# The odd slots' groups of x are loaded from ScalarE's queue, the even ones from SyncE's

## The chip, the cores and the metric

The kernel runs on one core of one Trainium2 chip. The metric is the device time of one execution in microseconds (us); what is compared is the median of several executions.

## The reference: what is computed

The input x has 1024 samples of 12500 numbers (float32, 51.2 MB). The reference is a factorization machine with a small network beside it:

```python
x_reg = input_data @ W_lin.T + b_lin                     # 1024 x 1
emb = input_data @ factors                               # 1024 x 16
sum_squared = jnp.square(emb.sum(axis=1))
squared_sum = (jnp.square(input_data) @ jnp.square(factors)).sum(axis=1)
h = jax.nn.relu(emb @ W1.T + b1)                         # 128 wide
h = jax.nn.relu(h @ W2.T + b2)                           # 64 wide
dnn_out = h @ W3.T + b3
x = x_reg + 0.5 * (sum_squared - squared_sum)[:, None] + dnn_out
x = 0.5 + jax.nn.sigmoid(x) * 5.0
```

Every number of x is needed twice: as it is, against 17 columns of weights (16 factors and W_lin), and squared, against one column of weights (the sums of the squared factors).

## The kernel before, in words

x comes transposed, 12500 rows of 1024 samples. It is read once, in this order: 128 first rows (xf), 84 remaining rows (xl), then 22 groups of 512 rows (2 MB each), then 1024 last rows (xe) in six pieces (PIECES, line 38: 1024, 1024, 1024, 512, 256 and 256 KB). In a group each of the 128 partitions gets 4 rows of x in one run of 16 KB (CHUNKS = 4); in a piece of xe it gets runs of 2 KB per row and half of the samples, so 8, 8, 8, 4, 2 and 2 KB.

The groups go through a ring of four slots of xr (RING = 4, group g in slot g % 4). The loops are written as 5 rounds of four slots (ROUNDS = 5; round 0 stands ahead of the loop, rounds 1 to 4 are the loop) and a rest of two groups, 20 and 21 (PART = 2). For each group:

- SP issues its load (line 172) into the slot of group g - 4. It waits for lin_used (TensorE has multiplied g - 4) and for squared (ScalarE has squared g - 4). The first four loads (line 166) wait for nothing. After the last load SP issues the six pieces of xe (line 184) with no wait at all, since xe has memory of its own.
- TensorE multiplies the group by its weights (multiply, line 426: 16 matmuls into p_lin) and then adds the fourth chunk of the squares of the group before (squares_before, line 416: 16 matmuls into p_tot).
- ScalarE squares the group into one of two buffers sq (square, line 234: two instructions at line 242 of 128 x 2048). It waits for the landing, and for VectorE and TensorE to be done with the squares of g - 2.
- VectorE adds three of the four chunks of squares, weighted, to acc (line 341).
- GpSimd copies the weights of the group into the ring wr (lines 196 and 204).

Each engine takes the groups in their order. At the start ScalarE's queue issues the loads of the weights w, of the last weights and of params (lines 223 to 225); after that only SP's queue is used. After group 21 TensorE's order is written out by hand (lines 517 to 550): the pieces of xe one after the other, and between them the squares, the two layers of the network and the sums for the two halves of the samples. The two stores of y (line 189) are SP's.

Of the kernel before, what the change touches and what calls it, by code (L numbers as in the profile page):

```python
# [22 lines left out]
RING = 4  # L23
# [3 lines left out]
PART = GROUPS - ROUNDS * RING  # L27
# [29 lines left out]
def fm_kernel(nc, xT, x_end, w_all, w_last, params, out):  # L57
    x_first = xT[0:P, :]
    x_rest = xT[P:P + REST, :]
    x_groups = xT[P + REST:, :].rearrange("(g p c) b -> g p (c b)", p=P, c=CHUNKS)  # L60
    out_rows = out.rearrange("(h t b) -> h t b", h=2, t=4)

    with ExitStack() as ctx:
        def sb(name, shape, dt=F32):
            return ctx.enter_context(nc.sbuf_tensor(name, shape, dt))
# [4 lines left out]
        def sem(name):  # L70
            return ctx.enter_context(nc.semaphore(name))
# [3 lines left out]
        xr = sb("xr", [P, RING, CHUNKS, B])  # L75
# [32 lines left out]
        x_landed = [sem(f"x_landed{s}") for s in range(RING)]  # L108
# [11 lines left out]
        squared = sem("squared")  # L120
        first_squared = sem("first_squared")
        added = sem("added")
        lin_used = sem("lin_used")
# [19 lines left out]
        def group(r, s):  # L143
            return RING * r + s

        def adds_by(g, c):

            return 2 + ADDS * g + c + 1
# [4 lines left out]
        def end_sq(h, c, n):  # L153

            return sq[:, h].rearrange("p c b -> p (c b)")[:, c * HALF:(c + n) * HALF]

        def by_vector(n):

            return 1 if n > 1 else 0

        @block.sync
        def _(sp):
            sp.dma_start(xf[:, :], x_first).then_inc(first_landed, 16)  # L163
            sp.dma_start(xl[0:REST, :], x_rest).then_inc(rest_landed, 16)  # L164
            for s in range(RING):
                sp.dma_start(xr[:, s].rearrange("p c b -> p (c b)"), x_groups[s]).then_inc(x_landed[s], 16)  # L166

            def load(r, s):

                sp.wait_ge(lin_used, group(r - 1, s) + 1)  # L170
                sp.wait_ge(squared, 2 * group(r - 1, s) + 2)
                sp.dma_start(xr[:, s].rearrange("p c b -> p (c b)"),  # L172
                             x_groups[bass.ds(group(r, s), 1)].rearrange("g p n -> (g p) n")
                             ).then_inc(x_landed[s], 16)

            with sp.Fori(1, ROUNDS) as r:
                for s in range(RING):
                    load(r, s)
            for s in range(PART):
                load(ROUNDS, s)  # L180
            at = 0
            for i, (h, c, n) in enumerate(PIECES):
                rows = x_end[at:at + P * n * HALF].rearrange("(p m) -> p m", p=P)
                sp.dma_start(xe[:, h, c:c + n, :].rearrange("p c b -> p (c b)"), rows).then_inc(end_landed[i], 16)
                at += P * n * HALF

            for h in range(2):
                sp.wait_ge(y_ready, h + 1)
                sp.dma_start(out_rows[h], y[0:P:32, h, :]).then_inc(y_stored, 16)
            sp.wait_ge(y_stored, 32)  # L190
# [30 lines left out]
        @block.scalar  # L221
        def _(act):
            act.dma_start(w[:, :, :].rearrange("p c k -> p (c k)"), w_all).then_inc(w_landed, 16)
            act.dma_start(wl[0:REST, :], w_last).then_inc(wl_landed, 16)
            act.dma_start(pr[:, :], params).then_inc(pr_landed, 16)

            act.wait_ge(zero_set, 1)
            nc.scalar.activation(warm[:, :], zero[:, 0:1], ACT.Sigmoid)  # L228
            act.wait_ge(first_landed, 16)
            nc.scalar.activation(sqf[:, :], xf[:, :], ACT.Square).then_inc(first_squared, 1)  # L230
            act.wait_ge(rest_landed, 16)
            nc.scalar.activation(sql[0:REST, :], xl[0:REST, :], ACT.Square).then_inc(first_squared, 1)

            def square(r, s):
                g = group(r, s)
                act.wait_ge(x_landed[s], 16 * (r + 1))
                if type(r) is not int or g >= SQ:

                    act.wait_ge(added, adds_by(g - SQ, ADDS - 1))
                    act.wait_ge(sq_used, g - SQ + 1)  # L240
                for c in range(0, CHUNKS, 2):
                    nc.scalar.activation(sq[:, s % SQ, c:c + 2, :], xr[:, s, c:c + 2, :],  # L242
                                         ACT.Square).then_inc(squared, 1)

            for s in range(RING):
                square(0, s)
            with act.Fori(1, ROUNDS) as r:
                for s in range(RING):
                    square(r, s)
            for s in range(PART):  # L250
                square(ROUNDS, s)

            def square_end(i):
                h, c, n = PIECES[i]
                n -= by_vector(n)
                act.wait_ge(end_landed[i], 16)
                if c == 0:

                    g = GROUPS - SQ + h
                    act.wait_ge(added, adds_by(g, ADDS - 1))  # L260
                    act.wait_ge(sq_used, g + 1)
                nc.scalar.activation(end_sq(h, c, n), xe[:, h, c:c + n, :].rearrange("p c b -> p (c b)"),  # L262
                                     ACT.Square).then_inc(end_squared, 1)

            def copy_lin(h):
                act.wait_ge(p_lin_done, h + 1)
                for u in range(2):
                    nc.scalar.copy(lin[:, h, u, :], p_lin[h][:, u * QUART:(u + 1) * QUART]).then_inc(lin_ready, 1)  # L268

            def layer1(h):  # L270
                act.wait_ge(p_h1_done, 2 * h + 1)
                nc.scalar.activation(h1[:, h, 0, :], p_h1[0][:, 0:QUART], ACT.Relu,
                                     bias=pr[:, C_B1:C_B1 + 1]).then_inc(h1a_ready, 1)

            def layer2(h):
                act.wait_ge(p_h2_done, 2 * h + 1)
                nc.scalar.activation(h2[0:H2, h, :], p_h2[0:H2, 0:QUART], ACT.Relu,  # L277
                                     bias=pr[0:H2, C_B2:C_B2 + 1]).then_inc(h2a_ready, 1)

            def embedding_square(h):  # L280
                act.wait_ge(p_es_done, h + 1)
                nc.scalar.activation(gsq[:, h, :], p_es[:, 0:EIGHTH], ACT.Square).then_inc(gsq_ready, 1)

            def sigmoid(h):
                act.wait_ge(p_tot_done, h + 1)
                nc.scalar.activation(sg[:, h, :], p_tot[h][:, 0:EIGHTH], ACT.Sigmoid,  # L286
                                     bias=bias[:, :]).then_inc(sg_ready, 1)

            square_end(0)
            square_end(1)  # L290
            copy_lin(0)
            act.wait_ge(pr_landed, 16)
            square_end(2)
            layer1(0)
            embedding_square(0)
            square_end(3)
            layer2(0)
            square_end(4)
            act.wait_ge(bias_ready, 1)
            sigmoid(0)  # L300
            copy_lin(1)
            layer1(1)
            embedding_square(1)
            layer2(1)
            sigmoid(1)
# [287 lines left out]
```

## Time and profile before

| | us |
|---|---|
| median of 3 executions | 141.06 (140.56 to 141.28) |
| the profiled execution | 141.34 |
| its span, first to last instruction on the core | 139.6 |
| TensorE matmuls busy | 91.5 |
| VectorE busy | 96.8 |
| ScalarE busy | 94.6 |
| GpSimd busy | 19.8 |
| moved by DMA | 52.26 MB, mean 374 GB/s over the span |

The profiled execution is one of its own, 0.28 us above the median; 1.74 us of it lie outside the span. Busy times are sums over the span. In the rows below the engines are PE (TensorE's matmuls), PEld (its weight loads), DVE (VectorE), ACT (ScalarE), POOL (GpSimd) and SP (SyncE); a q behind the name means the engine's instruction queue, where DMAs are issued. L172 is line 172 of the kernel.

### The profile page before, as it was taken

To read this page: it belongs to the slowest core of one execution; us is meant where nothing else is said; L and a number is where in the kernel's file an instruction comes from. 1 tells how busy PE (TensorE), PEld (TensorE's weight loads), DVE (VectorE), ACT (ScalarE), POOL (GpSimd) and SP (SyncE) were. 2 spreads that over 40 slices of the span, in tenths; PEclk is the share of its full clock that TensorE was granted. 3 is DMA by queue.
4 is the path that set the end of the run, shared out by engine and by line. 5 is a ranking of instruction groups with operands and counts; after the bars stand their busy time and mean duration, and the time that the engine had idled before them with its cause. 6 is when DMAs were issued, how large, how long until landed. Compare 5 with 4: busy or idle time off the path is not lost.

```text
span 139.6 us, 2634 instructions
## 1 busy us (share of the span) xinstructions
PE 91.5 (66%) x989; PEld 30.8 (22%) x989; DVE 96.8 (69%) x86; ACT 94.6 (68%) x65; POOL 19.8 (14%) x48
## 2 busy tenths in 40 slices
PE   6067852972964655964765647576574772999991
PEld 1010111220221211220221212112121120446650
DVE  0063798779678739778777977977797797796321
ACT  3050876966886656876696687669669776997341
POOL 0053002012022203022120220312022000000000
PEclk9999999599599685698698697579779789689999
DMA  4999999999999999999999999999999999992000
GB/s 89 377 371 412 446 418 418 441 432 404 432 446 418 418 437 434 399 437 446 413 418 451 423 409 446 441 409 427 446 413 418 451 425 402 423 396 79 5 8 1
DMA packets 4683, 52.26 MB, mean 374 GB/s; under 512 B 616, under 2 KB 752, under 8 KB 1476
## 3 DMA queue, kind: packets, MB, share of 16 engines
q1 hardware_dynamic: 4290, 51.21, 87.3%
q10 hardware_dynamic: 386, 0.95, 2.4%
q8 instruction: 5, 0.08, 0.2%
q14 instruction: 2, 0.02, 0.0%
HBM read 52.15 MB, written 0.00 MB: 374 GB/s over the span
## 4 chain that ended last, share of the span: by engine, by line
DMA 69%; ACT 14%; PE 12%; SPq 1%; issue 1%; ACTq 0%; DVE 0%
DMA xr<-in_xT 69%; ACT sq L242 13%; PE p_tot L392 5%; PE p_lin L392 5%; PE p_h L475 2%; PE p_h L506 1%; ACT sg L286 1%; PE p_es L485 0%; SPq L164 0%; ACT h L277 0%; SPq L163 0%; SPq L166 0%; SPq L172 0%; ACT lin L268 0%; DVE y L374 0%
## 5 line engine op out<-in xcount | busy, mean ns | idle before, releaser
L242 ACT ACTIVATE sq<-xr 128x2048 f32<-128x2048 f32 x44 | 81.6, 1903 | 30.0 <-DMA xr<-in_xT 29.0
L341 DVE SCALAR_TENSOR_TENSOR acc<-sq,wr,acc 128x1024 f32<-128x1024 f32 x66 | 84.9, 1286 | 23.2 <-ACT sq L242 20.6
L392 PE MATMUL p_lin<-xr,wr 128*17 128x512 f32 x352 | 57.4, 784 | 39.0 <-DMA xr<-in_xT 34.8
L204 POOL COPY wr<-s_all 128x4 f32 (+1 forms) x22 | 14.1, 639 | 74.4 <-PE p_tot L392 62.7
L392 PEld LDWEIGHTS p_lin<-xr,wr 128*17 128x17 f32 x352 | 9.5, 108 | 67.5 <-issue 41.5
L392 PE MATMUL p_tot<-sq,wr 128*1 128x128 f32 x352 | 17.4, 325 | 0.0
L392 PEld LDWEIGHTS p_tot<-sq,wr 128*1 128x1 f32 x352 | 11.9, 103 | 22.9 <-issue 22.1
L196 POOL COPY wr<-w 128x68 f32 (+1 forms) x22 | 6.8, 309 | 13.0 <-DMA w<-in_w_all 7.7
L392 PE MATMUL p_lin<-xf,w 128*17 128x512 f32 x4 | 3.6, 1052 | 4.9 <-DMA xf<-in_xT 4.9
L313 DVE SCALAR_TENSOR_TENSOR fsq<-w 128x1552 f32<-128x1552 f32 x1 | 1.8, 1776 | 7.0 <-DMA w<-in_w_all 7.0
L262 ACT ACTIVATE sq<-xe 128x1536 f32<-128x1536 f32 (+1 forms) x5 | 5.6, 1134 | 0.5 <-issue 0.5
L392 PE MATMUL p_lin<-xe,w 128*17 128x512 f32 (+2 forms) x48 | 5.3, 514 | 0.0
L230 ACT ACTIVATE sqf<-xf 128x1024 f32<-128x1024 f32 x1 | 1.1, 1058 | 4.6 <-DMA xf<-in_xT 4.6
L359 DVE SCALAR_TENSOR_TENSOR sq<-xe,s_all 128x512 f32<-128x512 f32 x5 | 3.7, 748 | 0.2
L392 PE MATMUL p_lin<-xl,wl 84*17 84x512 f32 x4 | 3.6, 1055 | 0.0
L392 PE MATMUL p_tot<-sq,s_all 128*1 128x128 f32 x88 | 3.3, 273 | 0.0
L369 DVE TENSOR_SCALAR h<-p_h,pr 64x256 f32<-64x256 f32 x2 | 1.0, 490 | 3.3 <-PE p_h L506 3.3
L228 ACT ACT_TABLE_LOAD x1 | 1.3, 1283 | 2.3 <-issue 2.3
L392 PEld LDWEIGHTS p_tot<-sq,s_all 128*1 128x1 f32 x88 | 2.3, 84 | 1.6 <-issue 1.0
L277 ACT ACTIVATE h<-p_h,pr 64x256 f32<-64x256 f32 x2 | 0.9, 468 | 2.5 <-PE p_h L506 2.5
L475 PE MATMUL p_h<-lin,pr 128*128 128x256 f32 x8 | 2.3, 405 | 0.1
L374 DVE TENSOR_SCALAR y<-sg 128x128 f32<-128x128 f32 x2 | 0.5, 226 | 2.2 <-ACT sg L286 2.2
(43 smaller groups left out, 27.7 us busy)
## 6 DMA issues: line engine op xcount, KB each, us to landing
xr<-in_xT SPq DMA_DIRECT2D x22, 2048.0 KB, 15.6
xe<-in_x_end SPq DMA_DIRECT2D x3, 1024.0 KB, 19.7
w<-in_w_all ACTq DMA_DIRECT2D x1, 824.5 KB, 7.4
xf<-in_xT SPq DMA_DIRECT2D x1, 512.0 KB, 7.6
xe<-in_x_end SPq DMA_DIRECT2D x1, 512.0 KB, 22.5
xe<-in_x_end SPq DMA_DIRECT2D x2, 256.0 KB, 22.8
xl<-in_xT SPq DMA_DIRECT2D x1, 336.0 KB
pr<-in_params ACTq DMA_DIRECT2D x1, 101.5 KB, 12.5
```

What stands on the lines that cost most here:

```text
L196: nc.gpsimd.tensor_copy(wr[:, s, :, 0:LIN], w[:, bass.ds(at, CHUNKS), :]).then_inc(wr_ready, 1)
L204: nc.gpsimd.tensor_copy(wr[:, s, :, LIN:WC].rearrange("p c k -> p (c k)"), s_all[:, bass.ds(at, CHUNKS)]).then_inc(wr_ready, 1)
L228: nc.scalar.activation(warm[:, :], zero[:, 0:1], ACT.Sigmoid)
L242: nc.scalar.activation(sq[:, s % SQ, c:c + 2, :], xr[:, s, c:c + 2, :], ACT.Square).then_inc(squared, 1)
L262: nc.scalar.activation(end_sq(h, c, n), xe[:, h, c:c + n, :].rearrange("p c b -> p (c b)"), ACT.Square).then_inc(end_squared, 1)
L286: nc.scalar.activation(sg[:, h, :], p_tot[h][:, 0:EIGHTH], ACT.Sigmoid, bias=bias[:, :]).then_inc(sg_ready, 1)
L313: nc.vector.scalar_tensor_tensor(fsq[:, :, :], w[:, :, 0:EMB], -0.5, w[:, :, 0:EMB], ALU.mult, ALU.mult).then_inc(fsq_ready, 1)
L341: nc.vector.scalar_tensor_tensor(acc[:, :], sq[:, s % SQ, c, :], wr[:, s, c, LIN:WC], acc[:, :], ALU.mult, ALU.add).then_inc(added, 1)
L359: nc.vector.scalar_tensor_tensor(end_sq(h, c, 1), xe[:, h, c, :], s_all[:, W_END + c:W_END + c + 1], xe[:, h, c, :], ALU.mult, ALU.mult).t ...
L392: return nc.tensor.matmul(out, lhsT, rhs, start=False, stop=False, skip_group_check=True)
L475: nc.tensor.matmul(p_h1[u][:, 0:QUART], pr[:, C_W1:C_W1 + H1], lin[:, h, u, :], start=True, stop=True).then_inc(p_h1_done, 1)
L506: nc.tensor.matmul(p_h2[u * H2:(u + 1) * H2, 0:QUART], pr[:, C_W2:C_W2 + H2], h1[:, h, u, :], start=True, stop=True).then_inc(p_h2_done, 1)
```

## The change

The nine loads of the odd slots that lie in the ring (groups 5, 7, 9, ... 21) are taken from SP and issued by ScalarE. SP keeps the even slots (groups 4, 6, ... 20), and behind them, as before, xe. On ScalarE the refill of slot 1 stands after the square of slot 2, the refill of slot 3 after the square of slot 0 of the next round; each waits for the same two counts as before. All else is as it was.

```diff
--- before.py
+++ after.py
@@ -173,10 +173,11 @@
                              x_groups[bass.ds(group(r, s), 1)].rearrange("g p n -> (g p) n")
                              ).then_inc(x_landed[s], 16)
 
+
             with sp.Fori(1, ROUNDS) as r:
-                for s in range(RING):
+                for s in range(0, RING, 2):
                     load(r, s)
-            for s in range(PART):
+            for s in range(0, PART, 2):
                 load(ROUNDS, s)
             at = 0
             for i, (h, c, n) in enumerate(PIECES):
@@ -242,11 +243,25 @@
                     nc.scalar.activation(sq[:, s % SQ, c:c + 2, :], xr[:, s, c:c + 2, :],
                                          ACT.Square).then_inc(squared, 1)
 
-            for s in range(RING):
+            def load(r, s):
+
+                act.wait_ge(lin_used, group(r - 1, s) + 1)
+                act.wait_ge(squared, 2 * group(r - 1, s) + 2)
+                act.dma_start(xr[:, s].rearrange("p c b -> p (c b)"),
+                              x_groups[bass.ds(group(r, s), 1)].rearrange("g p n -> (g p) n")
+                              ).then_inc(x_landed[s], 16)
+
+            for s in range(3):
                 square(0, s)
+            load(1, 1)
+            square(0, 3)
             with act.Fori(1, ROUNDS) as r:
-                for s in range(RING):
-                    square(r, s)
+                square(r, 0)
+                load(r, 3)
+                square(r, 1)
+                square(r, 2)
+                load(r + 1, 1)
+                square(r, 3)
             for s in range(PART):
                 square(ROUNDS, s)
```

## Rows read from the trace of the kernel before

**Rows 1.** The page, busy times by engine and the DMA slices.

```profile
PE 91.5 (66%) x989; PEld 30.8 (22%) x989; DVE 96.8 (69%) x86; ACT 94.6 (68%) x65; POOL 19.8 (14%) x48
DMA  4999999999999999999999999999999999992000
```

**Rows 2.** By stretches: length, busy (x instructions) per engine, PE clock, DMA share, GB/s.

```profile
40.00:66.00 26.00, 15.80 (x164) 4.79 (x156) 19.51 (x16) 18.65 (x11) 4.97 (x10) 0.79 1.00 423
66.00:92.00 26.00, 17.35 (x172) 5.41 (x168) 19.83 (x16) 20.08 (x12) 4.86 (x10) 0.76 1.01 432
```

**Rows 3.** ScalarE in order of time: start, length, instructions, idle before and its releaser.

```profile
64.93 3.71 ACT L242 ACTIVATE sq<-xr 128x2048 f32<-128x2048 f32 x2 [1.21 <-DMA xr<-in_xT]
...
118.62 3.71 ACT L242 ACTIVATE sq<-xr 128x2048 f32<-128x2048 f32 x2 [1.19 <-DMA xr<-in_xT]
```

**Rows 4.** The chain that ended last, its end: start, length, what.

```profile
102.96 15.64 DMA xr<-in_xT
...
118.64 2.52 PE p_lin L392 x16
...
137.33 0.23 DVE y L374
```

**Rows 5.** Pieces of xe: issues, first and last one's landing, first and last multiplication.

```profile
103.35 2.80 SPq L184 DMA_DIRECT2D xe<-in_x_end  x6
...
DMA to landing us min/median/max: 17.7/17.7/17.7
...
DMA to landing us min/median/max: 22.8/22.8/22.8
...
121.77 1.77 PE L392 MATMUL p_lin<-xe,w 128*17 128x512 f32 x8
...
132.28 0.41 PE L392 MATMUL p_lin<-xe,w 128*17 128x128 f32 x8
```

**Rows 6.** The start: issues in time, landings (page, part 6; last: first group of x).

```profile
0.74 0.40 ACTq L223 DMA_DIRECT2D w<-in_w_all  x1
0.75 0.40 SPq L163 DMA_DIRECT2D xf<-in_xT  x1
...
1.72 2.38 SPq L166 DMA_DIRECT2D xr<-in_xT  x4
1.88 0.35 ACTq L225 DMA_DIRECT2D pr<-in_params  x1
...
w<-in_w_all ACTq DMA_DIRECT2D x1, 824.5 KB, 7.4
xf<-in_xT SPq DMA_DIRECT2D x1, 512.0 KB, 7.6
pr<-in_params ACTq DMA_DIRECT2D x1, 101.5 KB, 12.5
...
DMA to landing us min/median/max: 12.9/12.9/12.9
```

**Rows 7.** TensorE in time: one group at full clock, one mostly at half.

```profile
59.98 1.91 PE L392 MATMUL p_lin<-xr,wr 128*17 128x512 f32 x16 [0.95 <-DMA xr<-in_xT]
61.71 0.62 PE L392 MATMUL p_tot<-sq,wr 128*1 128x128 f32 x16
...
86.67 1.11 PE L392 MATMUL p_tot<-sq,wr 128*1 128x128 f32 x16
...
99.15 3.49 PE L392 MATMUL p_lin<-xr,wr 128*17 128x512 f32 x16 [2.55 <-DMA xr<-in_xT]
```

**Rows 8.** Stretches at the start and the end, columns as in rows 2.

```profile
1.50:2.00 0.50, 0.50 (x2) 0.15 (x1) 0.00 (x0) 0.00 (x0) 0.00 (x0) 1.00 1.36 158
...
116.20:139.60 23.40, 17.96 (x320) 9.41 (x320) 13.13 (x17) 14.26 (x20) 0.00 (x0) 0.93 0.44 179
119.90:123.20 3.30, 3.30 (x32) 1.21 (x28) 2.47 (x2) 3.30 (x3) 0.00 (x0) 0.50 1.00 415
128.00:128.50 0.50, 0.50 (x20) 0.39 (x16) 0.09 (x1) 0.50 (x2) 0.00 (x0) 1.00 0.01 4
```

## Prediction

> **What bounds the kernel now.** I read the page's slices first: the DMA row stands at 9 or more from the second slice to the 36th, while VectorE and ScalarE are at 69% and 68% [rows 1]. Then the table by stretches: in the four stretches of 26 us from 14 to 118 us the DMA engines move 423 to 432 GB/s, and their share is never under 1.00 [rows 2]. Third, ScalarE's instructions in order of time: it squares each group for 3.71 us and then waits 1.15 to 1.2 us for the next one, so groups of 2 MB land every 4.89 us ((118.62 - 64.93) / 11) [rows 3]. The chain of waits says the same and adds the end: up to 118.6 us it is transfers of x, from then on TensorE, piece on piece, with ScalarE and VectorE in between, to 137.3 us [rows 4]. TensorE shows no idle there worth the name, and the pieces of the last rows (xe) have landed before it gets to them: the first is there at 103.35 + 17.7 = 121.05 us and is multiplied at 121.77; the last is issued at 103.35 + 2.80 - 0.43 = 105.7, is there 22.8 us later at 128.5 and is multiplied at 132.28 [rows 5]. So two things set the time: whether the DMA engines ever stand idle, and **when group 21, the last group of x, lands** (118.6 us). What follows that landing takes 18.9 us and moves with it.
>
> **The change, part by part.**
>
> *What is removed and added.* SP loses 9 of its 18 loads inside the ring (groups 5, 7, ... 21); ScalarE gets them, each as two waits and one issue. An issue occupied ScalarE's queue for 0.40 us for w and 0.35 for params [rows 6]. Nine times 0.4 is 3.6 us on ScalarE. It idles about 1.2 us per group, 2.4 us per pair of groups [rows 3], and the load stands after the second of the pair, so I price it at 0; without that idle it would be at most 3.6 us. The two waits are for squares that ScalarE itself has finished and for TensorE's multiplications of a group that landed a whole group earlier: TensorE needs 1.91 us at full clock and 3.4 to 3.5 us at half for them [rows 7], less than 4.89, so they too cost 0.
>
> *What moves.* In the old order the slot of group g is refilled when g has been squared. An odd slot is now refilled one group later: 7 after square 4, 9 after square 6, and so on, at the same moment at which SP refills the even slot. So loads go out in pairs, (7,8), (9,10) ... (19,20), 21 alone. Before, three loads were under way at each issue and a load took 15.6 us to land [rows 4]; now about two are.
>
> *How two queues share the DMA engines.* Only the start of the trace shows it. w and xf are issued at 0.74 and 0.75 us on different queues, both in 128 rows (824.5 KB and 512 KB, so 6.4 and 4 KB a row), and land 7.4 and 7.6 us later: together, although one is 1.6 times the other. params (0.8 KB a row) is issued at 1.88 and lands 12.5 us later at 14.4; the first group of x (16 KB a row), issued at 1.72, lands 12.9 later at 14.6 [rows 6]. Two transfers with the same number of rows end together whatever their bytes: the engines take turns row by row. By equal bytes params would have been through some 6 us earlier. I take turns by rows.
>
> *Steady state.* The members of a pair have 128 rows each, so they land together, every 2 x 4.89 = 9.78 us. Does the queue run dry? A pair lands at 0; ScalarE squares both, 7.45 us; its waits and those of SP add 0.15; then a latency L passes around the moving of bytes; and the new pair needs 9.78 us to move. That pair is due two periods later, at 19.56 (it is (g+3, g+4), with (g+1, g+2) between). So 17.4 + L must stay under 19.56, or L under 2.2 us. The rows bound L: the first bytes move in the half microsecond from 1.5 to 2.0, about 1.0 us after the issue, and the last ones between 128.0 and 128.5, when the last piece lands [rows 5, 8]: together some 1.5 us for the slowest of the engines. Counted by mean bytes the other end is higher: from 116.2 us to the end the stretch moves 23.4 x 179 = 4.19 MB, which is all of xe, so the mean engine is through with group 21 at 116.2, and it lands at 118.6: a lag of 2.4, which with the 1.0 makes L = 3.4 [rows 4, 8]. But in the half microsecond before the last landing 4 GB/s still move [rows 8], a hundredth of the full rate: one engine or a few are some 2 us behind the others, and it is the slowest, never dry itself, that sets a landing. So I take L = 1.5 and 0 us of empty queue, with 0.7 us in hand per pair, and keep (3.4 - 2.2) x 4 = 4.8 us as the other end (19.56 us is one cycle of the ring; there are four).
>
> *The end.* SP no longer waits for group 21: right after group 20 it issues all of xe, so xe stands in SP's queue behind 20 while 21 stands in ScalarE's behind 19. Groups 19 and 20 land together when all bytes up to 20 have moved, as before at 118.6 - 4.9 = 113.7 us. Then 21 (128 rows of 16 KB) takes turns with the first piece of xe (128 rows of 8 KB): 3072 KB have to move for both to be through, 1.5 x 4.89 = 7.33 us. Group 21 lands at 121.05 us: **+2.4 us**. The bound below is 0 (21 goes first, as now), the bound above 2.4 more (equal bytes, two pieces beside it: 2 x 4.89 after 113.7 is 123.5).
>
> *Is TensorE ready by then?* It gets 19 and 20 at once. A group costs 1.91 + 0.62 = 2.5 us at full clock and 3.4 + 1.1 = 4.5 us at half [rows 7]: it is through at 118.8 or at 122.7, so between 0 and 1.6 us late at 121.05. The trace alternates between the two levels, group by group, which gives 120.7: 0. ScalarE is through at 113.7 + 7.45 = 121.15: 0.1 late. I take 0.4 for both. After that the 18.9 us of [rows 4] follow unshortened; pieces of xe that lie ready earlier don't help, since TensorE was busy anyway.
>
> Here a rule of the Trainium skill speaks against any change in bandwidth: "DMA: Bandwidth & Descriptors", section "Issuing engines are not separate DMA queues", says that issuing from several engines only saves the sequencer's issue time. The traces agree as far as 1.00 of share leaves nothing to win [rows 2]; the order of arrival, on which my sum rests, that rule leaves open.
>
> *Sum.* The profiled execution took 141.34 us for a span of 139.6. 141.34 + 2.4 + 0.4 = 144.1; it lies 0.28 above the median of 141.06, so against the median **143.9 us**.
>
> **The rivals.**
>
> *Equal bytes* (chance 0.13): +2.4 more at the end, 146.3 us. For it: nothing but simplicity; against it params and w [rows 6].
>
> *The ring runs dry* (0.17): L is nearer to 3.4 than to 1.5, because the engines' lead over one another, now covered by three loads in flight, is lost each time a pair is used up. It decides from L = 2.2. Price 1 to 4.8 us on top: 144.9 to 148.7, middle 146.8.
>
> *Whole transfers by turns, so no change* (0.15): if a queue keeps the engines for one whole transfer before the other gets its turn, then the members of a pair land 4.89 us apart as now, the late refill is still covered (at each issue two groups less ScalarE's 3.85 us and the latency, some 4 us of work, are queued), and group 21 has its turn before the second piece at the latest: 0 to +2.4, and with 19, 20 and 21 having been issued in the order of now mostly 0, so 141.1 us. Against it: params would then not have needed as long as a group of x [rows 6]. The same page, section "Queues, rings and completion order", has the engines change queues after a packet of typically 9 to 17 descriptors; with 8 rows and a completion per engine that would be a whole transfer of this kernel, and 141.1 us.
>
> *A faster end* (0.05): the time falls if group 21 is not later and TensorE is granted the full clock after it. It runs at half (1.2 GHz) from about 119.9 to 123.2 us [rows 8], 3.3 us of work that would take 1.65 at 2.4 GHz: 141.06 - 1.65 = 139.4 us. It decides only where 21 stays at 118.6 and TensorE has idled longer ahead of it. Nothing in the rows makes both likely.
>
> **How the numbers follow.** Forecast 0.50, equal bytes 0.13, dry ring 0.17, no change 0.15, faster 0.05. The forecast's own range is 142.9 (nothing but half of the delay is missed) to 145.3 (TensorE at half clock, 1.6 for 0.4). The range for 8 in 10 takes in the no-change case and reaches into the dry ring: 141.0 to 147.5. Half a percent is 0.7 us, about what a measurement of this kernel can tell. Under 140.4: the faster case and a little, 0.06. Within: the no-change case less its tail, 0.14. Above: 0.80.
>
> **What the profile after should show.** Landings of x in pairs: ScalarE squaring two groups back to back (7.4 us), then idle about 2.3 us, instead of 1.2 us after each. Group 4 is late (about +4 us), since 5 shares its time. The DMA row stays at 9. Group 21 squared from about 121.1; the first piece of xe landed by then, some 20 us after its issue around 101. DMA's last bytes stay where they are, near 128 us. The prediction is wrong if groups still come every 4.89 us (turns by transfer), if gaps show in the DMA row ahead of the landings of pairs (L too small), or if 21 lands at 123.5 (equal bytes).

## The result, and the profile after

| | before | after |
|---|---|---|
| median, us | 141.09 (140.56 to 141.28, 4 runs) | 142.88 (142.46 to 143.49, 4 runs) |
| the profiled execution, us | 141.34 | 142.91 |
| its span, us | 139.6 | 140.8 |

The ratio is 1.0137, with a 95% interval of 1.0102 to 1.0171: 1.8 us slower, clear of noise. The forecast was 143.9 us with a range of 141.0 to 147.5.

The page of the kernel after, busy times and DMA slices, answers to [rows 1]:

```profile
PE 91.1 (65%) x989; PEld 30.5 (22%) x989; DVE 96.7 (69%) x86; ACT 94.3 (67%) x65; POOL 21.6 (15%) x48
DMA  4999999999999999999999999999999999980000
```

The table by stretches answers to [rows 2] (stretch, its length, busy time and instructions of each engine, PE clock, DMA share, GB/s):

```profile
40.00:66.00 26.00, 18.31 (x188) 5.93 (x180) 21.21 (x17) 20.82 (x12) 6.47 (x12) 0.79 1.00 424
66.00:92.00 26.00, 15.28 (x168) 4.84 (x172) 20.75 (x17) 19.19 (x11) 4.72 (x10) 0.86 1.01 432
```

Nothing is lost on the way: 424 and 432 GB/s for 423 and 432, the share is 1.00 or 1.01, no slice has a gap before the end. The bytes arrive as fast as before. What differs is whose bytes. ScalarE in order of time, kernel after, in the middle and at the end (as [rows 3]):

```profile
62.00 3.71 ACT L243 ACTIVATE sq<-xr 128x2048 f32<-128x2048 f32 x2 [1.17 <-DMA xr<-in_xT]
66.91 1.91 ACT L243 ACTIVATE sq<-xr 128x2048 f32<-128x2048 f32 x1 [1.20 <-DMA xr<-in_xT]
67.28 0.34 ACTq L250 DMA_DIRECT2D xr<-in_xT  x1
...
110.94 3.71 ACT L243 ACTIVATE sq<-xr 128x2048 f32<-128x2048 f32 x2 [1.16 <-DMA xr<-in_xT]
115.69 3.71 ACT L243 ACTIVATE sq<-xr 128x2048 f32<-128x2048 f32 x2 [1.05 <-DMA xr<-in_xT]
119.84 3.71 ACT L243 ACTIVATE sq<-xr 128x2048 f32<-128x2048 f32 x2 [0.43 <-PE p_tot L407]
```

Two things stand here that I hadn't expected. First, the load in ScalarE's queue (67.28) goes out 0.37 us after the square ahead of it has *begun*, not after it has ended at 70.6: the count that the load waits for was reached 1.2 us before the square began, and the queue runs ahead of the engine. The odd slot is refilled 1.6 us after its own square ended (62.00 + 3.71 = 65.7). Before, SP issued group 21's load at 102.96 ([rows 4]), 0.07 us after the square that it waited for, of group 17 (kernel before):

```profile
99.18 3.71 ACT L242 ACTIVATE sq<-xr 128x2048 f32<-128x2048 f32 x2 [1.15 <-DMA xr<-in_xT]
```

So the refill is 1.5 us later than it was, not a whole group. Second, the groups therefore don't arrive in pairs. They come every 4.9 us as before; the two queues are half a group apart, each with its own group half moved when the other one's lands. The trace's records of single DMA packets, of which each is one row of a group, show it: when the last row of group 20 had moved (114.56 us), 69 of the 128 rows of group 21 had moved too.

They are late by half a group, though, from group 8 on: group 10 is squared from 66.91, before from 64.93 [rows 3] (2.0 us, and about half a microsecond more without the late start explained below). At the end that lag has a price. Group 20 is in at 115.65 instead of 113.7 us, and 21 has come before 20 is dealt with. VectorE and TensorE in order of time show what that does; first the kernel before, then the kernel after (start, length, instructions, idle before):

```profile
115.73 4.06 DVE L341 SCALAR_TENSOR_TENSOR acc<-sq,wr,acc 128x1024 f32<-128x1024 f32 x3 [0.77 <-ACT sq L242]
120.62 4.07 DVE L341 SCALAR_TENSOR_TENSOR acc<-sq,wr,acc 128x1024 f32<-128x1024 f32 x3 [0.83 <-ACT sq L242]
124.61 2.31 DVE L359 SCALAR_TENSOR_TENSOR sq<-xe,s_all 128x512 f32<-128x512 f32 x3
...
125.41 0.40 PE L392 MATMUL p_tot<-sq,ones 128*1 128x128 f32 x8
```

```profile
117.69 8.26 DVE L356 SCALAR_TENSOR_TENSOR acc<-sq,wr,acc 128x1024 f32<-128x1024 f32 x6 [0.79 <-ACT sq L243]
125.87 2.07 DVE L374 SCALAR_TENSOR_TENSOR sq<-xe,s_all 128x512 f32<-128x512 f32 x3
...
123.69 0.62 PE L407 MATMUL p_tot<-sq,wr 128*1 128x128 f32 x16 [1.00 <-ACT sq L243]
...
126.67 0.40 PE L407 MATMUL p_tot<-sq,ones 128*1 128x128 f32 x8 [0.85 <-DVE sq L374]
...
138.59 0.23 DVE L389 TENSOR_SCALAR y<-sg 128x128 f32<-128x128 f32 x1 [0.88 <-ACT sg L301]
```

After, the additions of groups 20 and 21 are one row of six without a gap. VectorE's product of the first piece of xe starts 1.26 us later (125.87 for 124.61), TensorE waits 0.85 us for it, and from there all is 1.26 us later to the last instruction (138.59 for 137.33 in [rows 4]). In front of it TensorE, which bounded the old end, now has 1.00 + 0.85 = 1.85 us of idle. The 1.00 is ScalarE's: it squares 20 and 21 nearly back to back, too.

The chain of waits of the kernel after names another cause:

```profile
101.41 24.17 DMA xe<-in_x_end
125.63 0.24 issue
125.87 0.75 DVE sq L374
```

It follows VectorE's product back to a piece of xe that landed at 125.58. But VectorE shows no idle there; it was adding until 125.95. Nor does its first product read that piece: it needs the first one, which was in at 100.47 + 20.1 = 120.6, and the one of 125.58 is the third. A wait that ends while its engine is busy with something else is no cause.

1.26 us of the span against 1.8 us of the medians: the profiled execution of before had a late start. Its first group was squared from 14.62 us; among the thirteen kernels profiled here, variants with unchanged starts included, that instruction began between 13.86 and 14.62, mostly near 14.0, and at 14.07 in the kernel after. The 0.55 us belong to the executions, not to the change; 1.26 + 0.55 = 1.8. A profile that started at 13.89 us, of a kernel with all loads on SP and the time of the kernel before (late refill in one queue, below), gives the same without that addition:

```profile
113.36 3.71 ACT L242 ACTIVATE sq<-xr 128x2048 f32<-128x2048 f32 x2 [1.02 <-DMA xr<-in_xT]
124.24 2.30 DVE L359 SCALAR_TENSOR_TENSOR sq<-xe,s_all 128x512 f32<-128x512 f32 x3
136.95 0.23 DVE L374 TENSOR_SCALAR y<-sg 128x128 f32<-128x128 f32 x1 [0.88 <-ACT sg L286]
```

Beside it the kernel after squares group 20 2.33 us later (115.69), starts VectorE's product 1.63 us later (125.87) and its last instruction 1.64 us later (138.59).

### The profile page after: what moved, and what is told of

Same layout as the page of the kernel before. It is cut to its first block, busy times and chain, and to the rows that moved or that the text cites. A ratio compares the mean times of both kernels' runs of the same rounds, so it can differ in the third digit from the quotient of the medians.

```text
span 140.8 us, 2636 instructions
## 1 busy us (share of the span) xinstructions
PE 91.1 (65%) x989; PEld 30.5 (22%) x989; DVE 96.7 (69%) x86; ACT 94.3 (67%) x65; POOL 21.6 (15%) x48
## 4 chain that ended last, share of the span: by engine, by line
DMA 73%; ACT 9%; PE 7%; issue 5%; SPq 2%; ACTq 2%; DVE 1%; DVEq 0%
DMA xr<-in_xT 55%; DMA xe<-in_x_end 17%; ACT sq L243 8%; PE p_tot L407 3%; PE p_h L490 2%; ACTq L250 1%; PE p_lin L407 1%; PE p_h L521 1%; SPq L185 1%; DVE sq L374 1%; ACT sg L301 1%; SPq L172 0%; PE p_es L500 0%; ACT h L292 0%; SPq L164 0%
## 5 line engine op out<-in xcount | busy, mean ns | idle before, releaser
L205 POOL COPY wr<-s_all 128x4 f32 (+1 forms) x22 | 14.7, 667 | 76.2 <-PE p_tot L407 53.7
L407 PEld LDWEIGHTS p_tot<-sq,wr 128*1 128x1 f32 x352 | 11.6, 103 | 24.0 <-issue 22.4
L197 POOL COPY wr<-w 128x68 f32 (+1 forms) x22 | 8.1, 368 | 11.3 <-DMA w<-in_w_all 7.3
L407 PE MATMUL p_lin<-xe,w 128*17 128x512 f32 (+2 forms) x48 | 4.5, 451 | 0.0
L407 PE MATMUL p_tot<-sq,ones 128*1 128x128 f32 x40 | 2.0, 272 | 0.8 <-DVE sq L374 0.8
## 6 DMA issues: line engine op xcount, KB each, us to landing
xr<-in_xT SPq DMA_DIRECT2D x13, 2048.0 KB, 15.6
```

The lines of the kernel that those rows point to most:

```text
L197: nc.gpsimd.tensor_copy(wr[:, s, :, 0:LIN], w[:, bass.ds(at, CHUNKS), :]).then_inc(wr_ready, 1)
L205: nc.gpsimd.tensor_copy(wr[:, s, :, LIN:WC].rearrange("p c k -> p (c k)"), s_all[:, bass.ds(at, CHUNKS)]).then_inc(wr_ready, 1)
L407: return nc.tensor.matmul(out, lhsT, rhs, start=False, stop=False, skip_group_check=True)
```

## The experiments

**The refill really a group late (late refill).** ScalarE's load waits for the square ahead of it, which is what I had taken the change to do.

```diff
-                act.wait_ge(squared, 2 * group(r - 1, s) + 2)
+                act.wait_ge(squared, 2 * group(r - 1, s) + 4)
```

> ScalarE's load waits for the square that stands ahead of it in the program (the group after the one whose slot it refills), so that the odd refill really goes out a whole group late, at the moment of the even one, as my prediction had assumed of the change itself. Turns by rows and the prediction's sum: from group 7 on the groups land in pairs 9.8 us apart, ScalarE squares two back to back and idles 2.3 us, group 20 lands where it does before the change (113.7), group 21 at about 121.0, the end 2.4 to 2.9 us later than before: 143.5 to 144.0 us. Rival, equal bytes: 21 at 123.5, 146 us. Rival, the ring runs dry: gaps in the DMA row before a pair lands, over 145 us. Rival, lateness of the refill is of no effect: groups every 4.9 us and 142.9 us as with the change.

Measured: 154.1 us, ratio 1.093 (1.087 to 1.099). The page's DMA slices of this kernel:

```profile
DMA  4999999999999999799999899999599999960000
```

and its ScalarE in order of time:

```profile
83.94 0.37 ACTq L250 DMA_DIRECT2D xr<-in_xT  x1
86.61 3.71 ACT L243 ACTIVATE sq<-xr 128x2048 f32<-128x2048 f32 x2 [2.86 <-DMA xr<-in_xT]
90.48 3.71 ACT L243 ACTIVATE sq<-xr 128x2048 f32<-128x2048 f32 x2 [0.15 <-PE p_tot L407]
94.39 0.36 ACTq L250 DMA_DIRECT2D xr<-in_xT  x1
```

The pairs are there, two squares back to back; but a pair comes every 11.2 us (from 53.6 to 120.6 us six times), not every 9.8, and the slices show holes. The dry ring came true. The forecast of 143.9 us stood on a picture of the kernel that, once built, takes 154.1: 13 us more than the kernel before.

**Lateness without a second queue.** All loads on SP, the odd ones a group late.

```diff
-                sp.wait_ge(squared, 2 * group(r - 1, s) + 2)
+                sp.wait_ge(squared, 2 * group(r - 1, s) + (4 if s % 2 else 2))
```

> The kernel before, all on SP's queue, with the odd slots' loads a whole group late, as in the kernel with the late refill: they wait for the square of the next group too. So only the lateness is tried, without a second queue. In one queue the odd group still moves alone: issued at 3.85 us after a landing, it needs at most 3.4 + 4.9 us and is due 14.7 us after that landing. Theory: lateness alone costs nothing, 141.1. Rival: thinner cover of the DMA engines costs what the late refill cost on two queues (13 us) or a part of it: over 143.

Measured: 141.07 beside 140.81 us, ratio 1.0008 (0.9984 to 1.0033). Lateness alone is free. It costs 13 us only together with the second queue.

**A group alone, and two at once.** Each load waits until every group ahead of it is squared:

```diff
-                sp.wait_ge(squared, 2 * group(r - 1, s) + 2)
+                sp.wait_ge(squared, 2 * group(r - 1, s) + 8)
```

> The kernel before, but each load waits until all groups ahead of it are squared, so that a group of 2 MB moves while nothing else does. From issue to landing it then takes the moving, 4.89 us, and the latency L. My prediction took L = 1.5 us: 6.4 us. The other end of its range, L = 3.4: 8.3 us. The time of the kernel has no meaning beyond that (some 215 to 250 us).

Measured: 269.7 us, and from the issue of a load of line 172 to its landing (the line's instructions, kernel with lone groups):

```profile
DMA to landing us min/median/max: 7.8/8.0/8.4
```

8.0 - 4.9 = 3.1 us: twice the latency that the forecast took, and near its other end. Then pairs of an even and an odd group, issued together with nothing else under way, from one queue and from two:

```diff
-                sp.wait_ge(squared, 2 * group(r - 1, s) + 2)
+                sp.wait_ge(squared, 2 * group(r - 1, s) + (6 if s % 2 else 8))
```

> The kernel before, with the loads of an even group and the odd group behind it both held back until every group ahead of the two is squared, so that two groups are issued together while nothing else moves, both from SP's queue. With the latency of 3.1 us that a lone group showed: the even one lands 8.0 us after its issue, the odd one 4.9 later, 12.9 (12.6 after its own issue). The time of the kernel itself has no meaning.

> The same pairs, the even group from SP's queue and the odd one from ScalarE's. Turns by rows: both land together, 9.8 + 3.1 = 12.9 us after the issue, the even one 4.9 us later than from one queue. If two queues in step move their bytes more slowly, which would explain why the kernel with the late refill took 11.2 us per pair where I reckon 10.3 to 10.6: both land later than the second of the single queue by 0.5 us or more, 13.4 to 14.5.

For the two queues the odd loads are ScalarE's, with the waits of the pairs, each placed ahead of the squares of its own pair:

```diff
-                act.wait_ge(squared, 2 * group(r - 1, s) + 2)
+                act.wait_ge(squared, 2 * group(r - 1, s) + 6)
```

Measured, time from issue to landing, min/median/max: one queue, line 172, all 18 loads (the kernel took 203.7 us), then two queues, line 172 (even, SP) and line 250 (odd, ScalarE), nine each (237.3 us):

```profile
DMA to landing us min/median/max: 7.8/10.2/12.5
```

```profile
DMA to landing us min/median/max: 12.4/12.7/12.9
...
DMA to landing us min/median/max: 12.6/12.8/13.0
```

From one queue the first group is in after 7.8 us and more and the second about 4.9 us later. From two queues both need 12.7: the first one loses 4.9 us and the second gains nothing. The bytes of two queues in step move no slower than those of one (both in after 12.4 to 13.0 us; in one queue the second up to 12.5 after its own issue, which follows the first's by 0.7), so that is not what stretched the late refill's pairs to 11.2 us. By these numbers two periods there are 7.45 + 0.15 + 0.5 (ScalarE's wait for TensorE) + 12.7 = 20.8 us, 10.4 a pair. In its own trace the late refill's loads took longer, 14.3 us in the median (line 172, 12.1 to 18.1), which gives 22.4 us, the measured 11.2 a pair. That pair does not move alone: the one issued at 83.94 went out while the pair ahead, in at 86.6, was still moving. How the extra 1.6 us arise in detail stays open.

The packet records show the turns directly. While both queues had a group under way (181 to 189 us in the kernel with pairs from two queues), 106 rows from SP's queue and 105 from ScalarE's were finished.

**Whose turn it is.** The odd groups as four transfers of one chunk each, 4 KB a row instead of 16 (the first loads of slots 1 and 3 and the waits for landings are changed to match):

```diff
-                act.dma_start(xr[:, s].rearrange("p c b -> p (c b)"),
...
+                for c in range(CHUNKS):
+                    act.dma_start(xr[:, s, c, :],
+                                  x_groups[bass.ds(group(r, s), 1)].rearrange("g p n -> (g p) n")[:, c * B:(c + 1) * B]
+                                  ).then_inc(x_landed[s], 16)
```

> The changed kernel with each odd group loaded in four transfers of one chunk each, 128 rows of 4 KB instead of 16 KB; the even ones keep 16 KB. The bytes are the same. Turns by rows: while both queues have work SP's takes four times the bytes of ScalarE's; even groups land early (20 near 110, before its predecessor) and odd ones late, 21 only near 127 to 128, after nearly all of xe: 149 to 152 us. Turns by equal bytes: nothing changes against the changed kernel but three more issues of 0.35 us per odd group: 143 to 144.

Measured: 154.7 us (one execution), 3 us above the range of turns by rows and 11 above that of equal bytes. The last even group landed 10.4 us after its issue (15.6 in the kernel after), the last transfer of group 21 after 18.9 us, and ScalarE shows the order (kernel with short rows):

```profile
120.36 7.50 ACT L246 ACTIVATE sq<-xr 128x2048 f32<-128x2048 f32 x4 [6.42 <-DMA xr<-in_xT]
131.02 3.71 ACT L246 ACTIVATE sq<-xr 128x2048 f32<-128x2048 f32 x2 [3.16 <-DMA xr<-in_xT]
```

Group 20 was in at 103.9 + 10.4 = 114.3, but had to wait for 19, which came at 120.3; 21 came at 131.0. Group 19's four transfers had been issued from 100.4 to 101.9, 20's at 103.9. The same bytes in shorter rows get a smaller share. Groups 20 and 21 came later than turns by rows had it (114.3 for near 110, 131.0 for 127 to 128), but 20 came ahead of 19, as it had it. The packet records bear the turns out: from 114 to 124 us, with pieces of xe in rows of 8 KB in SP's queue and rows of 4 KB in ScalarE's, 340 and 334 rows were finished. Equal bytes is refuted. The Trainium skill, "DMA: Bandwidth & Descriptors", section "Queues, rings and completion order", has an engine change queues packet by packet, a packet being typically 9 to 17 descriptors; a whole transfer of this kernel, 8 rows and a completion per engine, would fit into one. By that the first of two groups would land after 8 us; it took 12.7. For these transfers the traces speak for turns of a row.

**The odd loads of the end back on SP.** Groups 17, 19 and 21 are loaded by SP again, in order; 5 to 15 stay with ScalarE. SP's side:

```diff
+            for s in range(RING):
+                load(ROUNDS - 1, s)
+            for s in range(PART):
+                load(ROUNDS, s)
```

> The changed kernel, but groups 17, 19 and 21 are loaded by SP again, in order; 5 to 15 stay with ScalarE. If the change costs only by the order in which bytes arrive at the end, then 20 and 21 land at 113.7 and 118.6 as before, and the time is that of before, 141.1 (140.7 to 141.5). If two queues lose something all along the ring (rate, gaps, ScalarE's issues), two thirds of the 1.8 us stay: 142.3.

Measured: 141.10 beside 140.84 us, ratio 1.0016 (0.9991 to 1.0041). Six of the nine loads from ScalarE cost nothing. ScalarE is back in step at the end of this kernel:

```profile
114.00 3.71 ACT L245 ACTIVATE sq<-xr 128x2048 f32<-128x2048 f32 x2 [1.18 <-DMA xr<-in_xT]
118.89 3.71 ACT L245 ACTIVATE sq<-xr 128x2048 f32<-128x2048 f32 x2 [1.19 <-DMA xr<-in_xT]
```

Within the ring group 8 had been squared as late as 58.47 us (57.13 in the kernel after); half a group of lag is regained as soon as one queue orders the bytes again, since the engines had been moving the next group meanwhile.

**xe behind group 21.** The pieces of xe are issued from ScalarE's queue behind the load of 21, so that 21 shares with none of them.

```diff
+                act.dma_start(xe[:, h, c:c + n, :].rearrange("p c b -> p (c b)"), rows).then_inc(end_landed[i], 16)
```

> The changed kernel with the six pieces of xe issued from ScalarE's queue behind the load of group 21, no longer from SP's behind group 20. Group 21 then shares with nothing once 20 is in. Theory A, the late landing of group 20 (half a group late, 115.65 us) sets the end through VectorE's six additions for 20 and 21: 20 stays at 115.7, 21 lands 1.2 us earlier than with the change (118.1), and the end is at most 0.4 us earlier: 142.5 to 142.9. Theory B, the landing of group 21 sets the end: 1.2 us earlier, 141.6.

Measured: 143.11 us, ratio 1.0145 (1.0105 to 1.0185). Group 21 landed at 106.1 + 12.2 = 118.3, 1.0 us earlier than with the change (119.35), and nothing came of it: the time is 0.2 us above the range of theory A and 1.5 above theory B. VectorE in this kernel:

```profile
117.81 8.26 DVE L362 SCALAR_TENSOR_TENSOR acc<-sq,wr,acc 128x1024 f32<-128x1024 f32 x6 [0.92 <-ACT sq L238]
125.99 2.07 DVE L380 SCALAR_TENSOR_TENSOR sq<-xe,s_all 128x512 f32<-128x512 f32 x3
```

Again six additions on end from 2 us after group 20's landing. Theory B, by which the landing of 21 counts, is refuted for the changed kernel. That VectorE carries the lateness of 20 to the end is read from the traces; no run made its work lighter.

**Group 21 alone on ScalarE's queue.** The kernel before, with this one load moved:

```diff
+            act.wait_ge(squared, 2 * g + 2)
+            act.dma_start(xr[:, 1].rearrange("p c b -> p (c b)"), x_groups[g + RING]).then_inc(x_landed[1], 16)
```

> The kernel before, with the load of group 21 alone issued from ScalarE's queue (ahead of square 19, about 1.5 us later than before); 17 and 19 stay with SP. Turns by rows: 21 shares with the rest of 19 and with 20 and has its turns while they wait, so it lands at 115 to 117, and 20, behind 19 in the other queue, only at about 118.6, where 21 landed before. ScalarE and VectorE take 20 first and then have both groups ahead of them: VectorE's additions end about 4 us later (118.6 + 2.0 + 8.3 = 128.9 for 124.7). Theory A, the landing of 20 counts with two groups' work behind it: 145.0 (144.0 to 145.5). Theory B, the landing of group 21 alone sets the end: 141.1 or less.

Measured: 145.76 us, ratio 1.034 (1.031 to 1.038), 5.0 us over the kernel before and 0.3 us above the range of theory A. Landings from the issue, group 20 (issued at 97.7) and group 21 (issued at 103.7), in this kernel:

```profile
DMA to landing us min/median/max: 20.7/20.7/20.7
...
DMA to landing us min/median/max: 13.7/13.7/13.7
```

and its ScalarE and VectorE in order of time:

```profile
118.34 3.71 ACT L241 ACTIVATE sq<-xr 128x2048 f32<-128x2048 f32 x2 [4.85 <-DMA xr<-in_xT]
120.34 4.06 DVE L347 SCALAR_TENSOR_TENSOR acc<-sq,wr,acc 128x1024 f32<-128x1024 f32 x3 [4.60 <-ACT sq L241]
122.98 3.71 ACT L241 ACTIVATE sq<-xr 128x2048 f32<-128x2048 f32 x2 [0.93 <-PE p_tot L398]
```

Group 21 is in at 117.4, a microsecond earlier than it is before the change, and group 20 at 118.4, 4.7 us later. One moved load costs 5 us, nine cost 1.8: what counts is not how many loads change the queue but how far the group ahead has been pushed back.

**A piece of xe ahead of group 21, one queue.**

```diff
+                if i == 1:
+                    load(ROUNDS, 1)
```

> The kernel before, all on SP's queue, with one exchange: the first piece of xe (1 MB) is issued ahead of group 21. No second queue. Group 20 lands as before (113.7), 21 by 1 MB later, 118.6 + 2.4 = 121.0. If all that follows group 21 is rigid (18.9 us, as the prediction has it), the end comes 2.4 us later: 143.5. If TensorE or the others have slack behind it, less: with TensorE at full instead of half clock in the first 3 us up to 1.2 us of it come back, 142.3. If only group 20 counts: 141.1.

Measured: 143.41 us, ratio 1.0182 (1.0146 to 1.0218). 2.57 us for 1 MB that moves ahead of group 21: that part of the forecast holds, what follows group 21 is rigid as long as 20 was in time.

**The change once more**, beside the pairs.

> The changed kernel once more, for a narrower interval beside the variants: 1.8 us over the kernel before, 142.6 to 142.9. Whether it starts 0.5 us sooner than before (first group squared at 14.07 for 14.62) by chance or by the change is to be seen in its rows: by chance, as the start of the program is the same.

Measured: 142.89 beside 140.63 us, ratio 1.0138 (1.0104 to 1.0173). It started at 13.99 us, so the early start is no property of one execution of the changed kernel; that it is no effect of the change either, the variants with all loads on SP show (13.86 with the piece ahead, 13.89 with the late refill in one queue). Group 20 was squared from 115.80, 2.44 us later than in these two (113.36 in both).

No variant was faster than the kernel before. The nearest, the late refill in one queue and the end back on SP, are equal to it within 0.4%.

## Why the prediction was right, and where it was wrong

- *The direction, and DMA engines that never idle.* Right: 1.00 of share before and after, and six moved loads that cost nothing.
- *Turns by rows.* Right, by the pairs (12.7 us both) and the short rows. One of the two pillars was chance, though: w and xf landed within 0.2 us of each other [rows 6] only in the two profiles with the latest starts, this one and the pairs from one queue (7.3 and 7.5 us); in the kernel after w lands 7.0 us and xf 6.3 us after the issue. params (12.8 us, the first group 12.4) stands in both.
- *"An odd slot is now refilled one group later ... at the same moment".* This step failed. The load went out 0.37 us into the next square, 1.5 us later than before, not 4.9. No groups came in pairs. Only the late group 4 came as foretold (squared from 38.77 us, before from 34.20). The sign "groups still come every 4.89 us" came true, too, but not for the reason that stands beside it, turns by transfer: it tested when the loads go out, not how the queues share.
- *L = 1.5 us and 0 us of empty queue.* This term was sized wrong: alone a group shows 3.1 us, beyond the 2.2 at which I had said that the ring runs dry. With the refill as I took it, the kernel takes 154.1 us. Two errors hid each other: the ring would have run dry, had the refill been as late as I thought. That the time still fell into the range is in part luck.
- *+2.4 us for the landing of group 21.* The amount was right and stood at the wrong group. With queues half a group apart, all bytes up to 20 and half of 21's have to move before 20 is in: it lands half a group, 2.44 us, later than before (1.95 in the two profiles, plus the 0.5 of the start; 2.33 and 2.44 beside the profiles that started near 13.9). Group 21 then shares its second half with half of the first piece of xe: 115.65 + 1.5 x 2.44 = 119.3; it landed at 106.4 + 12.9 = 119.35, later than before by 0.75 (1.3 without the start).
- *0.4 us for TensorE and ScalarE that are not ready.* In place of it stands VectorE, which the forecast left out. Before, its product of the first piece of xe (begun at 124.61, 0.75 long) ended at 125.36 us and TensorE took it at 125.41: VectorE was as late as TensorE itself, and no idle said so. Now it has six additions on end: from the landing of 20 to their end 2.04 + 8.26 = 10.3 us, before 11.0 (113.7 to 124.69), of which 0.8 was its idle between the two groups. So 2.44 - 0.7 = 1.7 us are left of the 2.44. That is the measured 1.8 us to within 0.1, where the forecast had 2.4 + 0.4 = 2.8. Behind it stands a smaller lateness of ScalarE and TensorE, which a faster VectorE would not remove: TensorE takes ScalarE's squares of the first piece at 124.98 us, 0.33 later than before and 0.78 later than in the late refill in one queue (124.20).

So the cause is shown from two sides: with the last loads in order the cost is gone, and with 21 earlier but 20 as late it stays.

## What to carry to other kernels

A stream that keeps the DMA engines at 1.00 can't gain from a second queue, but it can lose by it: two queues share by turns, so each transfer finishes later for the sake of one that isn't needed yet, and only order, not rate, is changed. In the middle of this stream, with a ring of four, that was free as long as the refill went out 1.5 us late; with the refill a whole group late two queues cost 13 us where one queue cost nothing. It is paid at the end, where the consumer has no slack; keep the last transfers in one queue, in the order in which they are used. A load placed behind a ScalarE instruction did not wait for that instruction to be done: it went out once the instruction had started and its own waits were met. If it is to wait for the result, it needs a wait that says so.

## What the runs showed of the hardware that was not expected

- DMAs issued from ScalarE's queue go out while the ACTIVATE ahead of them runs: 0.37 us after its start (67.28 for 66.91), though their own count had been reached at 65.7.
- A load of 2 MB that moves alone takes 8.0 us from issue to landing, 3.1 more than the 4.9 that its bytes take in a stream.
- Two queues share the engines by rows: 106 rows of one beside 105 of the other in 8 us, and 340 of 8 KB beside 334 of 4 KB in 10 us. Rows of 4 KB beside rows of 16 KB get so much less that a group of 2 MB issued 2 us earlier landed 6 us later (19 at 120.3, 20 at 114.3 us, in the kernel with short rows).
